# The head of a gated cross-attention and expert kernel in another order: loads, projections and the second unit's shift

## The reference

```python
def _L0_xattn_ref(q, k, v, mask, Wq, bq, Wk, bk, Wv, bv, Wo, bo):
    query = _split_heads(q @ Wq.T + bq)
    key_ = _split_heads(k @ Wk.T + bk)
    value = _split_heads(v @ Wv.T + bv)
    scores = jnp.einsum('bhqd,bhkd->bhqk', query, key_) / jnp.sqrt(jnp.asarray(D_K, query.dtype))
    scores = jnp.where(mask == 0, jnp.asarray(NEG, scores.dtype), scores)
    attn = jax.nn.softmax(scores, axis=-1)
    ctx = jnp.einsum('bhqk,bhkd->bhqd', attn, value)
    ...
    return ctx @ Wo.T + bo

x = x + jnp.tanh(g_xattn[0]) * _L0_xattn_ref(_layernorm(x, axis=-1), ctx_1024, ctx_1024, mask_1x1xSxS2_if1, ...)
x = x + jnp.tanh(g_ffn[0]) * _L0_ffn_ref(_layernorm(x, axis=-1), ...)
x = x + jnp.tanh(g_xattn[1]) * _L1_xattn_ref(_layernorm(x, axis=-1), ctx_1024, mask_BxSxS2_fk0, ...)
x = x + jnp.tanh(g_ffn[1]) * _L1_ffn_ref(_layernorm(x, axis=-1), ...)
```

## Time and profile before

| | |
|---|---|
| median of 3 runs | 727.4 us (721.49 to 727.75) |
| span of the profiled execution, first to last instruction | 717.2 us |
| PE busy | 642.3 us (90%) |
| DVE busy | 487.9 us (68%) |
| ScalarE busy | 347.4 us (48%) |
| GpSimd busy | 253.6 us (35%) |
| start of values(0) on PE | 33.72 us |

### The profile page before, as it was taken

How to read it: one execution, slowest core, us unless ns; L and a number is a source line. 1 busy time by engine, 2 the same in 40 slices (tenths; PEclk the granted TensorE clock), 3 DMA queues, 4 the chain that set the end, 5 groups by cost and what they waited for, 6 DMA issues and landing times.

```text
span 717.2 us, 12893 instructions
## 1 busy us (share of the span) xinstructions
PE 642.3 (90%) x4636; PEld 540.1 (75%) x4636; DVE 487.9 (68%) x1276; ACT 347.4 (48%) x568; POOL 253.6 (35%) x270
## 2 busy tenths in 40 slices
PE   5978688999899999989989988999988987899996
PEld 4756376888678788877778876889877753899995
DVE  6897888666877867766766764648657884455552
ACT  4434255356456456456544624435364532575751
POOL 3455736778732211221121402011031422363642
PEclk9899999899999999999999999999999999999998
DMA  7403203335552234223433523435222154864700
GB/s 216 154 16 135 94 41 148 132 132 198 204 200 91 89 122 143 89 89 112 168 118 109 186 90 114 158 124 191 89 89 104 59 192 137 291 210 148 246 16 29
DMA packets 43481, 94.55 MB, mean 132 GB/s; under 512 B 3535, under 2 KB 24399, under 8 KB 42400
## 3 DMA queue, kind: packets, MB, share of 16 engines
q1 hardware_dynamic: 41360, 87.64, 35.3%
q0 software_dynamic: 2064, 6.16, 2.4%
HBM read 72.96 MB, written 21.04 MB: 131 GB/s over the span
## 4 chain that ended last, share of the span: by engine, by line
PE 63%; DVE 23%; issue 7%; ACT 2%; DMA 2%; POOL 1%; ACTq 0%; SPq 0%; DVEq 0%; POOLq 0%
PE psum L1618 43%; PE psum L2167 6%; PE psum L1696 2%; PE psum L1726 2%; PE psum L1690 2%; PE psum L1656 1%; DMA work<-in_w 1%; DVE work L990 1%; DVE x_all L1118 1%; PE psum L1663 1%; PE psum L1675 1%; DVE work L1102 1%; DVE work L1086 1%; POOL slots L2311 1%; PE psum L1733 1%
## 5 line engine op out<-in xcount | busy, mean ns | idle before, releaser
L1618 PE MATMUL psum<-arena 128*128 128x256 f32 (+1 forms) x2544 | 441.3, 332 | 27.4 <-DVE x_all L1118 9.4
L1618 PEld LDWEIGHTS psum<-arena 128*128 128x128 f32 x2544 | 380.4, 197 | 70.7 <-issue 9.1
L2207 POOL TENSOR_TENSOR diag<-neg_ident,work 128x1024 fp32r<-128x1024 f32 x32 | 60.9, 1904 | 220.8 <-DVE work L1049 220.8
L1102 DVE TENSOR_TENSOR work<-work,psum 128x512 f32<-128x512 f32 x64 | 43.9, 685 | 63.8 <-PE psum L1618 58.1
L629 ACT ACTIVATE arena<-work 128x512 fp32r<-128x512 f32 x64 | 40.3, 630 | 77.3 <-DVE work L1102 69.5
L1118 DVE SCALAR_TENSOR_TENSOR x_all<-psum,w_exp,x_all 128x256 f32<-128x256 f32 x128 | 55.8, 477 | 26.9 <-PE psum L1618 26.1
L622 ACT ACTIVATE work<-psum 128x512 f32<-128x512 f32 x64 | 38.2, 597 | 49.5 <-PE psum L1618 49.2
L1107 DVE TENSOR_TENSOR arena<-work,arena 128x512 fp32r<-128x512 f32 x64 | 49.1, 766 | 10.0 <-ACT arena L629 9.7
L597 ACT ACTIVATE work<-psum 128x1024 f32<-128x1024 f32 x32 | 32.8, 1025 | 32.0 <-PE psum L1696 31.8
L2167 PE MATMUL psum<-arena 128*128 128x256 f32 x384 | 47.9, 284 | 0.0
L1049 DVE TENSOR_REDUCE work<-psum 128x8 f32<-128x1024 f32 x32 | 39.0, 1218 | 12.5 <-PE psum L1675 12.4
(11 more groups left out here) (203 smaller groups left out, 854.8 us busy)
## 6 DMA issues: line engine op xcount, KB each, us to landing
arena<-kept SPq DMA_DIRECT2D x24, 1024.0 KB, 5.6
work<-in_w SPq DMA_DIRECT2D x16, 1024.0 KB, 7.8
kept<-arena SPq DMA_DIRECT2D x8, 1536.0 KB, 6.0
arena<-kept SPq DMA_DIRECT2D x24, 512.0 KB, 4.8
work<-in_w SPq DMA_DIRECT2D x8, 768.0 KB, 7.9
slots<-fill POOLq DMA_DIRECT2D x1, 2080.0 KB, 8.9
work<-in_ctxT SPq DMA_DIRECT2D x8, 256.0 KB, 3.4
work<-in_ctxT SPq DMA_DIRECT2D x4, 512.0 KB, 5.4
```

The costliest lines, as they stand in the source:

```text
L1102: dve.tensor_tensor(gu[i % 2], gu[i % 2], ps[:, UP, :], ALU.mult).then_inc(hm, 1)
L1618: mm = pe.matmul(dst, left(i, k), right(j, k), start=(n == 0), stop=(n == 3 * K2 - 1))
L2207: pool.tensor_tensor(diag, neg_ident[:, :].rearrange("p (o q) -> p o q", o=1).to_broadcast([P, 8, P]), mx[u % 2].rearrange("p (h o) -> p h ...
```

## The change

Five things are done in the head, and nothing behind sequence 0.

1. SP's queue: x of half 0 is issued first. The q weights, x of half 1 and the mask come ahead of the v weights and the context of half 1.
2. The low halves of the q and v weights are made by GpSimd (its own semaphore counts them), those of k and out by DVE. ScalarE makes the high ones in the order k, q, v, out.
3. PE transposes half 0 first, then k, q, transposes half 1, then the first scores. Both value projections come after unit 1's shift.
4. DVE makes the memsets of `values_ready` first, then the norm of half 0 ahead of the k weights' low half, and `k_low(0)`, `q_low(0)` ahead of `maximum(0)`; both `v_add` come after `maximum(2)`.
5. The pass b = 0 of the loop is written out. In it unit 1's hide, shifted scores and shift come ahead of unit 2's hide and scores for max. q of half 1 uses bank DN, the values bank UP.

```diff
+            x_load(0, 0, 2)
             ctx0_load(0)
             weights(1)
-            x_load(0, 0, 2)
             sp.dma_start(cst[:, :], const).then_inc(s_const, 16)
+            weights(0)
             sp.dma_start(biasc[:, :], bcols).then_inc(s_bias, 16)
-            weights(2)
-            weights(0)
-            ctx0_load(1)
             x_load(1, 2, 4)
             sp.dma_start(mask0_raw, mask0.rearrange("a p n -> p a n")).then_inc(s_mask0, 16)
+            weights(2)
+            ctx0_load(1)
             weights(3)
...
+            weights_high(1)
+            weights_high(0)
+            xn_high(0, TL)
             act.wait_ge(s_bias, 16)
             k_high(0, GA)
-            xn_high(0, TL)
             ctx_high(1)
-            act.wait_ge(s_setup.sem, 3)
+            weights_high(2)
+            act.wait_ge(s_setup.sem, SETUP_DIAGONAL)
             q_high(0, DN)
-            k_high(1, GA)
             xn_high(1, TL)
             weights_high(3)
+            k_high(1, GA)
...
-            weights_low(0)
+            values_ready()
             norm0(0)
+            weights_low(1)
             constants_ready()
-            weights_low(1)
-            weights_low(2)
+            masks_ready()
+            xn_low(0, TL)
+            norm0(1)
             dve.wait_ge(s_bias, 16)
             k_low(0, GA)
-            xn_low(0, TL)
-            norm0(1)
-            masks_ready()
-            maximum(0)
             dve.wait_ge(su.sem, su.last)
             q_low(0, DN)
+            maximum(0)
+            xn_low(1, TL)
+            maximum(1)
             k_low(1, GA)
-            xn_low(1, TL)
             weights_low(3)
-            values_ready()
+            bias_ready()
+            q_low(1, DN)
+            maximum(2)
             dve.wait_ge(s_small, 16 * 7)
             v_add(0, UP)
+            v_add(1, UP)
...
-            pe.wait_ge(s_wa_lo, 1)
-            k_project(0, GA)
             pe.wait_ge(s_const, 16)
             xn_transpose(0, TL)
-            pe.wait_ge(s_wa_lo, 2)
-            v_project(0, UP)
-            pe.wait_ge(s_wa_lo, 3)
+            pe.wait_ge(s_wko_lo, 1)
+            k_project(0, GA)
+            pe.wait_ge(s_wqv_lo, 1)
             q_project(0, DN)
-            pe.wait_ge(k_lo, 2)
-            pe.wait_ge(s_setup.sem, 6)
+            xn_transpose(1, TL)
+            pe.wait_ge(s_setup.sem, SETUP_ONES)
             hide_for_max(0)
             scores_for_max(0)
+            pe.wait_ge(k_lo, 2)
             k_project(1, GA)
-            xn_transpose(1, TL)
+            scores(0)
+            pe.wait_ge(q_lo, 2)
+            q_project(1, DN)
+            hide_shifted(1)
+            scores_shifted(1)
+            shift(1)
+            pe.wait_ge(s_wqv_lo, 2)
+            v_project(0, UP)
+            hide_for_max(2)
+            scores_for_max(2)
+            pe.wait_ge(v_ok, 1)
+            v_project(1, UP)
...
-            for b in range(GB):
+            for b in range(1, GB):
...
+            def weights_low(m):
+                pool.wait_ge(s_wa_hi, SPLIT_ORDER.index(m) + 1)
+                pool.tensor_tensor(wa[1][:, m, :, :], wa0_raw[:, m, :, :], wa[0][:, m, :, :], ALU.subtract).then_inc(s_wqv_lo, 1)
+
             ctx0_low(0)
+            weights_low(0)
             pool.wait_ge(s_const, 16)
-            pool.wait_ge(s_setup.sem, 3)
+            pool.wait_ge(s_setup.sem, SETUP_DIAGONAL)
             k_masks(0)
             ctx0_low(1)
+            weights_low(2)
             diagonals(0)
             k_masks(1)
```

More of the change, by code:

```diff
@@ L258, in block_kernel @@
         s_passed = sem("wait_passed")
-        ORDER0 = (1, 2, 0, 3)
         def reciprocal_root(dve, step, var, r, t):
@@ L277, in block_kernel @@
         s_setup = Steps(sem("vector_setup_step"), 0)
-        s_wa_hi, s_wa_lo = sem("attn_weights_high"), sem("attn_weights_low")
+        SETUP_DIAGONAL, SETUP_ONES = 7, 10
+        s_wa_hi = sem("attn_weights_high")
+        s_wko_lo, s_wqv_lo = sem("attn_k_and_out_weights_low"), sem("attn_q_and_v_weights_low")
+        SPLIT_ORDER = (1, 0, 2, 3)
         s_bo = sem("bias_gated")
@@ L657, in _, with weights_high @@
             ctx_high(0)
-            def weights_high(n):
-                m = ORDER0[n]
+            def weights_high(m):
                 act.wait_ge(s_waraw[m], 16)
                 act.activation(wa[0][:, m, :, :], wa0_raw[:, m, :, :], ACT.Copy).then_inc(s_wa_hi, 1)
-            for n in range(3):
-                weights_high(n)
+            weights_high(1)
+            weights_high(0)
+            xn_high(0, TL)
             act.wait_ge(s_bias, 16)
             k_high(0, GA)
-            xn_high(0, TL)
             ctx_high(1)
-            act.wait_ge(s_setup.sem, 3)
+            weights_high(2)
+            act.wait_ge(s_setup.sem, SETUP_DIAGONAL)
             q_high(0, DN)
-            k_high(1, GA)
             xn_high(1, TL)
             weights_high(3)
+            k_high(1, GA)
             act.wait_ge(s_small, 16 * 7)
@@ L685, in _ @@
                 if b == 0:
-                    act.wait_ge(s_wa_lo, 4)
+                    act.wait_ge(s_wqv_lo, 1)
+                    act.wait_ge(s_wko_lo, 1)
                 exponential(2 * b)
                 if b % 2 == 0:
-                    q_high(nxt, GA)
+                    q_high(nxt, GA if b else DN)
                 if b:
                     o_high(b - 1)
+                else:
+                    act.wait_ge(s_wqv_lo, 2)
+                    act.wait_ge(s_wko_lo, 2)
                 exponential(2 * b + 1)
@@ L947, in step @@
                 dve.wait_ge(vs.sem, vs.done(ins))
-            def weights_low(n):
-                m = ORDER0[n]
-                dve.wait_ge(s_wa_hi, n + 1)
-                dve.tensor_tensor(wa[1][:, m, :, :], wa0_raw[:, m, :, :], wa[0][:, m, :, :], ALU.subtract).then_inc(s_wa_lo, 1)
+            def weights_low(m):
+                dve.wait_ge(s_wa_hi, SPLIT_ORDER.index(m) + 1)
+                dve.tensor_tensor(wa[1][:, m, :, :], wa0_raw[:, m, :, :], wa[0][:, m, :, :], ALU.subtract).then_inc(s_wko_lo, 1)
             def constants_ready():
@@ L1237, in _ @@
                 maximum(2 * b + 1)
-                if b:
-                    o_normalise(b - 1)
+                o_normalise(b - 1)
                 if b % 2:
@@ L1243, in _ @@
                     q_low(nxt, GA)
-                if b:
-                    o_low(b - 1)
+                o_low(b - 1)
                 if b % 2:
@@ L1250, in _ @@
                     normalise0(nxt)
-                if b:
-                    residual(b - 1)
-                else:
-                    bias_ready()
+                residual(b - 1)
                 if b == 1:
@@ L1833, in second_piece @@
                     v_project(h, bank)
-            for b in range(GB):
+            for b in range(1, GB):
                 nxt = (b + 1) // 2 + 1
-                if b:
-                    values(b - 1)
+                values(b - 1)
                 if b > 1:
@@ L1841, in _ @@
                 scores(2 * b)
-                if b:
-                    o_transpose(b - 1)
+                o_transpose(b - 1)
                 if b % 2 == 0:
@@ L1846, in _ @@
                     first_piece(b, GA)
-                if b:
-                    o_back(b - 1)
+                o_back(b - 1)
                 scores(2 * b + 1)
-                if b:
-                    out_project(b - 1)
+                out_project(b - 1)
+                if b == 1:
+                    pe.wait_ge(k_lo, 4)
                 if b % 2:
```

1 line of the change is left out of this document (added).

## The result

| | before | after |
|---|---|---|
| median of the timed runs | 726.0 us (20 runs, 720.85 to 732.44) | 728.93 us (20 runs, 724.33 to 732.78) |
| ratio | | 1.0049, 95% interval 1.003 to 1.0069 |
| span of the profiled execution | 717.2 us | 730.1 us |
| mean granted clock of that execution | 0.973 | 0.961 |
| start of values(0) | 33.72 us | 37.81 us |

The change costs 2.9 us, 0.5%, which lies inside "no change within 1%". The forecast of 728.0 us is 0.9 us off, but not for the reasons given: values(0) was to start at 34.3 us and started at 37.81, and the tail, which was to be 683.5 us long, had 692.3. The two spans differ by 12.9 us, the medians by 2.9, so a pair of single executions overstates the difference. The time of an execution lies 1.8 us above its own span (731.9 and 730.1 us for the one shown here).

The account below looks back on a forecast made before the run. The engines' own work bounds the kernel (PE 63%, DVE 23% of the chain). 3.8 us won at shift(1), 4.4 us given back, values(0) +0.6 us: 717.2 + 0.6 + 10.2 = 728.0 us, range 721.0 to 731.0 us.

Parts of the forecast that it names:

- no change within 1%: Whole kernel: time within 1% of before, about 7.3 us, given a chance of 0.93.
- So the 2.4 us are gone by the first scores: Front: q_high(0) starts 2.4 us earlier, yet first scores for max start at 18.7 us, against 18.54 before.
- the hold on the second norm: DVE's second norm: GpSimd holds it between 0 and 2.1 us; it ends at 16.8 us, alone at 14.7.
- five pieces in a row: GpSimd beside the second norm: masks of k, ctx low and value weights' low half, busy from 12.0 to 16.6 us.
- The middle: First scores to shift(1): PE alone sets the pace; shift(1) at 27.8 us against 31.62, 3.8 us won.
- The give-back: shift(1) to values(0): v_project(1) waits for v_add(0) behind maximum(2); 6.5 us instead of 2.1, 4.4 us given back.
- The sum: values(0) at 34.3 us against 33.72, +0.6 us; 717.2 + 0.6 + 10.2 = 728.0 us.
- both of the signs: Forecast wrong if values(0) lies below 32 or above 36.5 us, or the tail behind it isn't about 683.5 us.
- the 10.2 us: Whole kernel: difference between the profiled span, 717.2 us, and the median, 727.4 us, carried unchanged.
- The small gain: Rival, second norm: the hold misses the normalisations, or the clock is luckier; 722 to 726.5 us, 0.29 together with kept gain.
- slower by the clock: Rival, head: PE's idle times let the clock level fall, so projections run slower; 729.5 to 732 us, chance 0.15.
- The gain is kept: Rival, before v_project(1): PE's wait for v_add(0) is short, 3.8 us stay, 724 us; 0.29 together with small gain.

Follow-up runs that it names:

- v_project(0) in the gap, masks held, even: Changed kernel with v_project(0) in PE's gap before xn_transpose(1) and GpSimd's masks of k held until the second norm ends, GpSimd's program length unchanged: 721.35 us, ratio 0.9953.
- v_project(0) in the gap: Changed kernel with v_project(0) behind q_project(0), value weights' halves made earlier, v_add(0) ahead of maximum(1): 721.45 us, ratio 0.9937.
- v_add(0) first: Changed kernel with v_add(0) ahead of maximum(2) on DVE, nothing else: 726.34 us, ratio 1.001.
- unit 2 back: Changed kernel with unit 1's hide, shifted scores and shift again between unit 2's hide and scores for max and the rest: 724.68 us, ratio 0.9978.
- masks held, even: Changed kernel with GpSimd's masks of k held until the second norm ends, by a wait replacing another, program length unchanged: 726.19 us, ratio 1.0008.
- PE kept busy: Changed kernel with 22 added matmuls of 128x512 in PE's idle time ahead of xn_transpose(1): 727.88 us, ratio 1.0016.
- first tokens third: Changed kernel with x of half 0 third again on SP's queue, behind the context and k weights: 729.28 us, ratio 1.007.
- held-back kernels: Changed kernel with GpSimd's masks of k held until the second norm ends: 732.96 us with an added wait, 726.19 us with the wait replacing another.
- early wait: Changed kernel with one more wait in GpSimd's program ahead of the masks of k, already satisfied when reached: 733.64 us, ratio 1.0102.

## Why the prediction was right, and where it was not

| profile | values(0), us | median, us |
|---|---|---|
| v_project(0) in the gap, masks held, even | 30.3 | 721.35 |
| v_project(0) in the gap | 31.2 | 721.45 |
| before (two profiles) | 33.7, 34.4 | 726.0 |
| v_add(0) first | 34.7 | 726.34 |
| unit 2 back | 35.3 | 724.68 |
| masks held, even | 35.4 | 726.19 |
| PE kept busy | 36.1 | 727.88 |
| first tokens third | 37.2 | 729.28 |
| changed kernel | 37.8 (same order: 36.5) | 728.93 |

The medians come from different batches, whose runs of before differ by 0.4 us.

**The first half.** The first tokens landed as predicted: the norm started at 3.51 us. It ended at 8.46 instead of 7.6, since GpSimd's ctx low held one operation (6.16, 1.15 us). q_high(0) began at 13.79 us, predicted 14.0. "So the 2.4 us are gone by the first scores" was too kind: 2.6 us were lost on top.

**The step that failed: the hold on the second norm.** I wrote "One scalar operation of the root is held about 1.0 us, and the two normalisations, due at 14.9, are held". The norm started 0.9 us late (11.62, behind the first hold, the mask's landing and L968, itself held), and then four operations of the root were held, in all 3.6 us instead of 2.1, so it ended at 19.14 us instead of 16.8. The held-back kernels show this as a cause: there the norm took 4.0 us, not 7.5. The row that I had of before showed one such operation held (14.00, 0.80 us); beside GpSimd's instructions in a row that had to be counted once for each, not once in all. (The prediction speaks of five pieces in a row, but lists four, and its 16.6 us is the sum of four; four it was.)

**The middle was right as a difference.** From the first scores to q·k of unit 0 I had 4.6 us, measured 4.68; the four masked copies took 1.13 us (predicted 1.30); q_project(1) ran at the full level (1.58 against 1.55); from shift(0) to shift(1) 3.44 us (3.6). shift(1) at 30.12 instead of 27.8 us is the norm's 2.3 us and nothing else: it moved up 1.5 us, not 3.8.

**The give-back was right in mechanism.** PE waited 1.92 us for v_add(0), predicted 1.9. From shift(1) to values(0) it was 6.58 us in the profile with the early wait, predicted 6.5; in the profile of after 7.69, because v_project(1) took 2.79 us in a low stretch. The run with v_add(0) first removed the wait and 2.6 us of time, to within 0.4 us of before's runs.

**The sum was right by two errors.** values(0) came at 36.5 to 37.8 us instead of 34.3, in one of the two profiles above the 36.5 us, and with a tail of 692.3 us. By both of the signs that I had named for it the forecast was wrong, and that its number came out was luck. Against before's 33.7 and 34.4 that is 2 to 4 us, and the medians say 2.9. I had +0.6, on a median of 727.4 us from three runs; 20 runs put it at 726.0. The base was 1.4 us too high and the change 2.3 us too small; the two cancel but for 0.9 us. The tail "683.5 us" belonged to a quick execution; the 10.2 us that I carried on top are 1.8 us around the span, and 8.4 us of difference between that execution and the median. Carried as one number they did no harm.

**The rivals.** The small gain did not come. The level did fall, twice: PE's gap of 5.7 us ahead of the second transposes, where I had reckoned with 3, brought the low stretch from 18 us, as the kernel with PE kept busy shows. The one at 35 us begins behind the gap for v_add(0), but the same gap of 1.92 us was followed by the full level in the profile with the early wait (v_project(1) in 1.69 us), so the gap alone doesn't decide. Of the 1.7 us that the first one took at shift(0) (24.77 against 26.47) only 0.84 was left at shift(1). So "slower by the clock" names a real effect with a small share at values(0). What I had said against it was weak: the wait "again ahead of 29.6" was of 0.14 us (29.51 to 29.65), and behind the one ahead of 24.96 the granted clock was 0.57. The larger share there is the hold and the wait for v_add(0). "The gain is kept" put 3.8 us on a short wait, though the wait is 1.9 of the 4.4 us given back; without it the kernel was 2.6 us faster.

Open is how much of the 2.9 us each of the two carries: taken away alone, the wait gave 2.6 us and the hold 2.7, together more than the loss, and no run took both away from the changed order.

## What to carry to other kernels

Before moving vector work beside GpSimd work, count for each side the instructions, not the microseconds: each GpSimd instruction in a row can hold one tiny vector operation for its whole length. When an order is changed, what was moved up is worth only what its follower can use; the gap that PE had anyway was the place for the projection, and filling it, with what had to move along, made the changed kernel 7.5 us faster. And compare the far end of the trace too: a head that is 2.3 us earlier and a time that is 4 us longer can both be true, when one instruction more in an engine's program brings a stall there.

## What the runs showed of the hardware that I had not expected

- A vector operation on two elements (161 ns) takes 1190 ns beside a row of GpSimd subtractions of 1.26 us; on one element (153 ns) it is free. A 128x512 subtraction on DVE goes from 0.69 to 1.63 us, and GpSimd's own instructions then come 1.67 us apart instead of 1.22.
- One wait more in GpSimd's program, satisfied some 4 us before it is reached, moved a stall without a releaser into the last expert layer 600 us later: 12.36 us, where the others wait 5.8 to 8.4 us for DVE, and 4.7 us in the time.
- Two executions of the same kernel before differ by 5.6 us in span (717.2 and 722.8), with the granted clock at 0.973 and 0.969 and the low stretches at other places; values(0) differs by 0.7 us only.
